# Keys made once and kept in device memory, instead of key-norm products and folded queries

## The reference, cut to what matters

```python
xn = layer_norm(x, g_norm)
q = xn @ Wq                                   # 128 -> 1024
k, v = jnp.split(ctx @ Wkv, 2, axis=-1)       # 128 -> 1024 each
q, k, v = map(split_heads, (q, k, v))         # 16 heads of 64
k = concat([null_key, k]); v = concat([null_value, v])
q = l2norm(q) * q_scale
k = l2norm(k) * k_scale
attn = softmax(einsum('bhid,bhjd->bhij', q, k) * 8.0)
out = einsum('bhij,bhjd->bhid', attn, v)
out = out.reshape(b, -1, 1024) @ Wout
return layer_norm(out, g_out)
```

## Time and profile before

| what | us |
|---|---|
| median of 3 runs | 1401.02 |
| profiled execution | 1405.52 |
| its span | 1403.7 |
| TensorE matmul busy | 1220.3 (87%) |
| DVE / ACT / POOL busy | 641.4 / 439.2 / 314.4 |
| mean granted TensorE clock | 0.892 of full |
| first to last key product, both cores | 50.5 to 524.2 |
| long block, first score product | at 803.3 |
| long block, end (copy of the last batch's output) | at 1321.2 |

### The profile page before, as it was taken

The page is one execution under the profiler, slowest core; times in us unless marked ns, Lnnn a source line. Parts: engine busy times, 40 slices in busy tenths (PEclk is TensorE's granted clock), DMA queues, the critical chain, the costliest instruction groups (busy, mean ns, idle before and its releaser), DMA issues.

```text
span 1403.7 us, 12934 instructions
## 1 busy us (share of the span) xinstructions
PE 1220.3 (87%) x4726; PEld 700.7 (50%) x4726; DVE 641.4 (46%) x1098; ACT 439.2 (31%) x550; POOL 314.4 (22%) x94
## 2 busy tenths in 40 slices
PE   7999578987779998776597899999999999999558
PEld 4666233744656662453486544454445444544534
DVE  2487573134459886222522343334334333433344
ACT  2466313331346552241110523322332232233011
POOL 0000000000000000000000066655663665566000
PEclk8999799985879998797588999999999999999569
DMA  8000000030000002005000000000000000000100
GB/s 349 42 1 1 0 0 0 1 120 0 1 0 1 0 1 90 0 1 224 1 1 0 1 15 19 19 16 16 19 19 12 19 19 16 15 19 7 64 3 7
DMA packets 21365, 40.02 MB, mean 29 GB/s; under 512 B 2496, under 2 KB 18880, under 8 KB 19648
## 3 DMA queue, kind: packets, MB, share of 16 engines
q1 hardware_dynamic: 21312, 39.30, 7.7%
HBM read 39.03 MB, written 0.26 MB: 28 GB/s over the span
## 4 chain that ended last, share of the span: by engine, by line
PE 80%; DVE 11%; ACT 6%; issue 2%; POOL 1%; DMA 0%; POOLq 0%; DVEq 0%; ACTq 0%
PE PSUM L1814 15%; PE PSUM L1818 15%; PE PSUM L1389 8%; PE PSUM L1460 3%; PE PSUM L1421 3%; PE PSUM L1398 2%; PE PSUM L1451 2%; PE PSUM L1549 2%; PE PSUM L1560 2%; PE PSUM L1415 2%; PE PSUM L1843 1%; PE PSUM L1849 1%; DVE ARENA L867 1%; PE PSUM L1924 1%; PE PSUM L1745 1%
## 5 line engine op out<-in xcount | busy, mean ns | idle before, releaser
L420 POOL TENSOR_TENSOR ARENA<-ARENA 128x2048 f32<-128x2048 f32 x64 | 288.7, 4512 | 196.2 <-ACT ARENA L654 196.2
L1230 DVE TENSOR_TENSOR ARENA<-PSUM,RK 128x512 f32<-128x512 f32 x256 | 175.7, 691 | 271.6 <-PE PSUM L1814 269.3
L1814 PE MATMUL PSUM<-ARENA,CK 128*128 128x512 f32 x512 | 257.3, 606 | 5.1 <-DVE ARENA L1230 4.3
L1818 PE MATMUL PSUM<-ARENA,CK 128*128 128x512 f32 x512 | 252.8, 597 | 5.8 <-ACT ARENA L676 3.7
L654 ACT ACTIVATE ARENA<-ARENA,CK 128x2048 f32<-128x2048 f32 x64 | 128.1, 2002 | 349.7 <-DVE ARENA L1230 349.7
L1818 PEld LDWEIGHTS PSUM<-ARENA,CK 128*128 128x128 f32 x512 | 97.6, 191 | 131.7 <-issue 113.2
L1814 PEld LDWEIGHTS PSUM<-ARENA,CK 128*128 128x128 f32 x512 | 97.6, 194 | 126.2 <-issue 97.7
L363 POOL TENSOR_TENSOR RSTD<-VE,MHALF 128x4 f32<-128x4 f32 x17 | 17.2, 1009 | 614.8 <-DVE VE L721 614.8
L1389 PE MATMUL PSUM<-WK,CT 128*128 128x512 f32 x256 | 122.9, 603 | 0.0
L450 ACT ACTIVATE SQ<-PSUM 128x512 f32<-128x512 f32 x128 | 76.3, 597 | 72.4 <-PE PSUM L1389 64.6
L743 DVE TENSOR_REDUCE RK<-SQ 128x8 f32<-128x512 f32 x128 | 84.1, 681 | 14.6 <-ACT SQ L450 12.5
(11 more groups left out here) (362 smaller groups left out, 1518.1 us busy)
## 6 DMA issues: line engine op xcount, KB each, us to landing
CT<-in_ctxT SPq DMA_DIRECT2D x4, 1024.0 KB, 10.4
CK<-in_l0f_experts SPq DMA_DIRECT2D x1, 4096.0 KB, 23.5
CK<-in_ctxk SPq DMA_DIRECT2D x1, 4096.0 KB, 12.5
ARENA<-in_l2f_experts SPq DMA_DIRECT2D x2, 2048.0 KB, 8.3
CK<-in_ctxT SPq DMA_DIRECT2D x64, 64.0 KB, 1.8
CK<-in_ctxr SPq DMA_DIRECT2D x64, 64.0 KB, 1.9
ARENA<-in_l2f_experts SPq DMA_DIRECT2D x1, 3072.0 KB, 14.3
WB<-in_wb SPq DMA_DIRECT2D x1, 2738.5 KB, 11.2
```

Source lines behind the costliest of these rows:

```text
L420: nc.gpsimd.tensor_tensor(LS[b % 2], LS[b % 2], PR[:, k % 2, :], ALU.add)\
L1230: ve.tensor_tensor(PR[:, k % 2, c * 512:(c + 1) * 512].rearrange("p (j n) -> p j n", j=4), PSUM[:, c % 2, :].rearrange("p (j n) -> p j n", ...
L1814: mm(bank(c % 2), CTT[:, k, :], qpb[:, b, c * 512:(c + 1) * 512], start=True, stop=True)\
L1818: return mm(bank(4 + c), CKT[:, k, :], PR[:, k % 2, c * 512:(c + 1) * 512], start=first, stop=final, skip_group_check=True)
```

## The change: what it does

The keys are now made, turned (feature on the partition, context row along the free axis), and kept.

- In the two cores, a key product is now weights by context (128 features of two heads x 512 rows). There are again 64 per core, but in the first 14 groups: five in each of the first eight, four in the next six (`key_plan`). The scalar engine copies each to one of four buffers, SP writes it to device memory (256 KB each, 32 MB in all), and GpSimd squares it. TensorE adds the squares over the partitions by products with a selection matrix: four products of 512 columns with 32 weight columns each, to four partition ranges of bank 0, for every four keys (`add_squares`), and turns the sums for every eight (`turn_norms`). The scalar engine copies them before and after. The vector engine has no part in it.
- In the long block, SP reads the keys back, 2 MB for every four tiles, into two buffers. A tile's scores are 16 products of 64 partitions and 128 columns, a pair of heads on partitions 0 to 63 and 64 to 127 writing to different banks. Value rows are made for each tile (two products of 128 x 512), copied half by the vector, half by the scalar engine. The values are summed by 16 products of 128 partitions and 128 columns with 64 weight columns, a pair of heads writing to partitions 0 to 63 and 64 to 127 of a bank. The exponential is done in two halves.
- The products with the folded key weights, the gather of raw rows, the value and turn steps at a batch's end and the raw tiles' DMAs are gone. A batch is closed by four products of 512 columns for the sums, two reciprocals of 512 and a multiplication of 1024 on the vector engine, and `Wout`. The null key is scored by 16 products of 512 columns ahead of the first tile, and its values open each batch's sum with four products of one partition.
- All loops are written out. The double norm becomes one statistic and two powers (`norm_twice_dve`). Some buffers move, and some signals share a name.

```diff
-    mm(bank(5 + 2 * c), CT[:, t * P:(t + 1) * P], WK[:, c * 512:(c + 1) * 512],
-        start=True, stop=True).then_inc(sem("key_rows"), PE.sends("key_rows"))
+def key_rows(units):
+    for n in units:
+        if n >= 2:
+            nc.tensor.wait_ge(sem("keys_kept"), n - 1)
+        mm(bank(5 + 2 * (n % 2)), WK[:, (n % 8) * P:(n % 8 + 1) * P], CT[:, (n // 8) * 512:(n // 8 + 1) * 512],
+           start=True, stop=True).then_inc(sem("key_rows"), PE.sends("key_rows"))
+def add_squares(halves):
+    for h in halves:
+        nc.tensor.wait_ge(sem("key_squares"), 4 * h + 4)
...
+        for j in range(4):
+            last = mm(PSUM[32 * j:32 * j + 32, 0, :], w("l3x_pick")[:, 32 * (h % 2):32 * (h % 2) + 32],
+                      KSQ[(4 * h + j) % 6], start=h % 2 == 0, stop=h % 2 == 1, skip_group_check=True)
...
+def key_squares(n0):                       # GpSimd
+    for n in range(n0, n0 + 64):
+        nc.gpsimd.wait_ge(sem("keys_kept"), n + 1)
+        if n >= 6:
+            nc.gpsimd.wait_ge(sem("key_squares_added"), (n - 6) // 4 + 1)
+        nc.gpsimd.tensor_tensor(KSQ[n % 6], KEEP_T[n % 4], KEEP_T[n % 4], ALU.mult)\
+            .then_inc(sem("key_squares"), PO.sends("key_squares"))
+def keep_keys(units):                      # scalar engine
+    for n in units:
+        nc.scalar.wait_ge(sem("key_rows"), n + 1)
+        if n >= 4:
+            nc.scalar.wait_ge(sem("key_squares"), n - 3)
+            nc.scalar.wait_ge(sem("dma_keys%d" % (n % 4)), 16 * (n // 4))
+        act(KEEP_T[n % 4], bank(5 + 2 * (n % 2)), ACT.Copy).then_inc(sem("keys_kept"), AC.sends("keys_kept"))
...
+def scores(t):                             # TensorE, long block
+    b, g = t // KEY_TILES, t // 4
+    if t % 4 == 0:
+        nc.tensor.wait_ge(sem("dma_keys_back%d" % (g % 2)), 16 * (g // 2 + 1))
+    for half in range(2):
+        if t:
+            nc.tensor.wait_ge(sem("l3x_scores_taken"), 4 * (t - 1) + 2 * half + 2)
+        for j in range(4):
+            c = 4 * half + j
+            for i in range(2):
+                last = mm(PSUM[:, 2 + 2 * half + i, j * P:(j + 1) * P],
+                          KG[DH * i:DH * (i + 1), g % 2, c, (t % 4) * P:(t % 4 + 1) * P],
+                          QSC[DH * i:DH * (i + 1), c, b * P:(b + 1) * P], start=True, stop=True)
+        last.then_inc(sem("l3x_scores"), PE.sends("l3x_scores"))
+def values(t):
+    nc.tensor.wait_ge(sem("l3x_probs"), 2 * t + 2)
...
+    for c in range(8):
+        for i in range(2):
+            at = ((c // 4) * 2 + i) * 512 + (c % 4) * P
+            last = mm(PSUM[DH * i:DH * (i + 1), 6 + c // 4, (c % 4) * P:(c % 4 + 1) * P],
+                      VT[:, t % 2, (2 * c + i) * DH:(2 * c + i + 1) * DH], PR[:, t % 2, at:at + P],
+                      start=False, stop=t % KEY_TILES == KEY_TILES - 1, skip_group_check=True)
+    last.then_inc(sem("l3x_values"), PE.sends("l3x_values"))
+scores(0)
+for t in range(TILES):
+    more = t + 1 < TILES
+    if more:
+        scores(t + 1)
+    if t > 1 and t % KEY_TILES == 1:
+        finish_out(t // KEY_TILES - 1)
+    if more:
+        value_rows(t + 1, 0)
+        value_rows(t + 1, 1)
+    if t and t % KEY_TILES == 0:
+        finish_sums(t // KEY_TILES - 1)
+    if t % KEY_TILES == 0:
+        null_values(t // KEY_TILES)
+    values(t)
...
+def finish_sums(b):                        # vector engine
+    nc.vector.wait_ge(sem("l3x_l"), b + 1)
+    ve.reciprocal(L9INV[:, 0:512], bank(0))
+    ve.reciprocal(L9INV[:, 512:1024], bank(1)).then_inc(sem("l3x_l_kept"), DV.sends("l3x_l_kept"))
+    nc.vector.wait_ge(sem("l3x_l_kept"), DV.sent("l3x_l_kept"))
+    nc.vector.wait_ge(sem("l3x_o_kept"), b + 1)
+    ve.tensor_tensor(OT8, OT8, L9INV, ALU.mult).then_inc(sem("l3x_o_ready"), DV.sends("l3x_o_ready"))
```

More of the change, by code:

```diff
@@ L305, in build, with key_plan, turn_of @@
         PICK2 = ARENA[0:16, 2048 + PAIRS * 3 * P:2048 + PAIRS * 3 * P + 16 * DH]
+        def key_plan(n0):
+            plan, n, added = [], n0, n0 // 4
+            for g in range(16):
+                first, second = (3, 2) if g < 8 else (2, 2) if g < 14 else (0, 0)
+                halves = list(range(added, n // 4))
+                halves = halves[:2 - added % 2]
+                turns = [h // 2 for h in (plan[-1][2] if plan else []) if h % 2]
+                plan.append((list(range(n, n + first)), list(range(n + first, n + first + second)), halves, turns))
+                added, n = added + len(halves), n + first + second
+            assert added == n // 4 and not plan[-1][2]
+            return plan
+        work_v, work_o = {}, {}
+        turns = [0]
+        def turn_of(table, at):
+            table[at] = turns[0] % 2
+            turns[0] += 1
+        turn_of(work_v, 0)
+        turn_of(work_v, 1)
+        for t in range(TILES):
+            if t > 1 and t % KEY_TILES == 1:
+                turn_of(work_o, t // KEY_TILES - 1)
+            if t + 1 < TILES:
+                turn_of(work_v, 2 * t + 2)
+                turn_of(work_v, 2 * t + 3)
+        turn_of(work_o, B - 1)
         block = ctx.enter_context(nc.Block())
@@ L453, in core_act @@
+            def core_act(groups, scale, plan=None):
                 for g in range(groups):
+                    first, second, halves, turned = plan[g] if plan else ([], [], [], [])
                     nc.scalar.wait_ge(sem("scores_shifted"), AC.due("scores_shifted"))
                     act(SX[:, g % 2, :], SX[:, g % 2, :], ACT.Exp, scale=scale).then_inc(sem("probs"), AC.sends("probs"))
[L456 to L457 removed]
+                    keep_norm_rows(turned)
+                    keep_keys(first)
@@ new lines, in _ @@
+            for t in range(TILES):
+                more = t + 1 < TILES
+                begins = more and (t + 1) % KEY_TILES == 0
+                ends = t and t % KEY_TILES == 0
+                if more:
+                    scale(t + 1, 0)
+                    scale(t + 1, 1)
+                if t and t % KEY_TILES == 1:
+                    finish_out(t // KEY_TILES - 1) if t > 1 else None
+                if more:
+                    value_rows(t + 1)
+                    scale(t + 1, 2)
+                    scale(t + 1, 3)
+                if begins:
+                    begin_sums((t + 1) // KEY_TILES)
+                if ends:
+                    finish_sums(t // KEY_TILES - 1)
@@ L1402, in core_pe @@
                 for g in range(groups):
+                    first, second, halves, turned = plan[g] if plan else ([], [], [], [])
                     if g + 1 < groups:
                         scores(g + 1)
-                    if norms_from is not None:
-                        key_norms_pe(norms_from + 4 * g, 2)
+                    turn_norms(turned)
+                    key_rows(first)
                     nc.tensor.wait_ge(sem("probs"), PE.due("probs"))
@@ new lines, in finish_sums @@
+            def finish_sums(b):
+                nc.tensor.wait_ge(sem("l3x_summed"), KEY_TILES * (b + 1))
+                take(0)
+                take(1)
+                for q in range(4):
+                    i = q % 2
+                    last = mm(PSUM[DH * i:DH * (i + 1), q // 2, :], w("ones")[:, 0:DH], LS[b % 2][:, q * 512:(q + 1) * 512],
+                              start=True, stop=True)
+                last.then_inc(sem("l3x_l"), PE.sends("l3x_l"))
+                freed[0] = freed[1] = ("l3x_l_kept", b + 1)
```

541 lines of the change are left out of this document (245 added, 296 removed).

## The result

The changed kernel takes 1354.95 us (median of 4 executions, 1347.57 to 1361.26) against 1401.03 for the kernel before (1400.99 to 1401.47). The ratio is 0.9668, with a 95% interval of 0.9618 to 0.9719. The profiled execution took 1356.67 us, its span 1354.6; the forecast for it was 1357, and 1353 for the median. Run again on another chip, the changed kernel took 1359.88 (1352.14 to 1362.19), the kernel before 1405.14 (1401.26 to 1409.51), ratio 0.9661 (0.9618 to 0.9705). So its spread of 10 us and more belongs to the kernel and not to one chip.

What follows compares the result with a forecast made beforehand. TensorE's stream was taken to bound the long block and both cores. The terms -65 - 22 - 9 - 4 - 3 + 29 + 26 = -48 gave 1357 us profiled, 1353 against the median of 1401.0; range 1308 to 1430.

Steps and rivals of the forecast that it cites:

- tile of the long block: Each long-block tile falls from 6.87 to 5.86 us, with short passes at 0.060 us each: -65 over 64.
- closing a batch: Long block, 3 times: sums and null values 3.8 us, TensorE waiting 5.2; together 9.0 against 16.2: -22.
- end: Long block, from the last addition to the end of the copy, 29.5 us before: -9.
- start: Long block's start: 15.6 us becomes 11.1, with null scores in pairs at 6.9: -4; unpaired +3.
- L0_xattn's core: Core's own work, keys, squares and turning 114.7 us, plus 5 of waits: 120 against 91, +29.
- L1_attn's core: This core, with changes between full and partial products, takes 121 us against 95: +26.
- The question on which all hung: Whether two TensorE products on different array halves run at once; overlap taken from a row showing only input-partition halves.
- Rival A: Products that differ only in their output partitions don't overlap: +141 us together, 1542; chance 0.15.
- Squares: In the cores, an addition takes 1.1 us and two changes between full and partial products, 1.3; 20.8 in all.
- Waits: In the cores, waits around GpSimd's squares and the scalar engine's copies: 0.3 us a group, 5 a core.
- C: Everything overlaps, but at 0.072 us a pass: long-block tile 6.62 us, kernel 1402; chance 0.15.
- D: In the cores, the ring of copy, square and addition binds: 20 us more in each, 1393; chance 0.06.

Runs made afterwards that it cites:

- the experiments on order: Changed kernel with only product order changed: scores half by half 1400.70 us, scores two by two 1366.11, value sums half by half 1439.62.
- the one on the squares' range: Changed kernel with the four products of each addition of squares all writing output partitions 0 to 31, not a range of 32 each: 1435.26 us.
- the fastest kernel: Changed kernel with closings spread over later tiles, last batch's end in halves with TensorE adding its probabilities, and a group's two additions of squares apart: 1329.82 us.
- the kernel with the additions apart alone: Changed kernel with a group's second addition of squares moved behind its value products, all squares on GpSimd: 1344.14 us.

## Why the prediction was right, point by point

| step | predicted | measured in the traces | |
|---|---|---|---|
| tile of the long block | 5.86 us, -65 | 5.80 us, -68 | short pairs ran at about 0.060 a pass |
| closing a batch | 9.0 us, -22 | 10.3, 8.6, 10.3 us, -19 | see below |
| end | 20.4 us, -9 | 18.6 us, -11 | see below |
| start | 11.1 us, -4 | 6.0 us, -10 | null scores 1.9 us and not 6.9 |
| double norms | -3 | -3.3 | |
| L0_xattn's core | +29 | +30.3 | |
| L1_attn's core | +26 | +31.4 | see below |
| sum | -48 | -50, and +1 in what is not named | the span fell by 49.1 |

The question on which all hung was answered as taken. Overlap across output partitions was chosen by the nearest row, though that row is of the other kind; the experiments on order and the one on the squares' range show that both kinds exist and what they are worth: 87 us for the values' half, 82 for the squares' quarters. Without either the kernel would have been slower than before. Rival A had been given 0.15, which was the risk of arguing from one kind to the other.

The answer was right for the two kinds of pair, but the total owes something to luck: single terms were off by up to 6 us, and they cancel.

*The closing.* Its 9.0 us left out the output products, 1.9 us at full clock, and took 5.2 us of waiting where 3.0 were measured (0.73 or 0.78, and 2.27); its own figures, 8 us less 2.4, give 5.5 or 5.6 rather than 5.2. Another 1.6 and 1.3 us are the half clock behind the wait, in two of the three.

*The end.* No run shows the 3.8 us at half clock that its 20.4 took for the sums: they took 1.94, at a granted clock of 1.00, which accounts for the 1.8 us between 20.4 and 18.6. The output products, behind a wait of 8.02 us, took 3.75 at 0.50.

*Squares.* 1.1 us and two mode changes, 1.3, was taken for an addition. It takes 1.0, and the change back shows in the two key products behind it, 1.91 us where two take 1.72 in the core's first group. So an addition costs 1.2 in all. By lines of the chain in L0_xattn's core, the additions have 16.2 us against the 20.8 forecast, the keys 58.0 against 55.0 (the changes back are in them), scores, transposes and values 37.8 against 35.5 (the first eight products of scores took 3.78 us in place of 2, at a granted clock of 0.50), the turning 3.6 against 3.4. The sum is 115.5 against 114.7, and it agrees in part because those 1.8 us at half clock made up for some of the squares.

*Waits.* 5 us a core were taken, 6.1 measured (122.61 - 116.48): 5.5 of them are the ring, as listed above, and 0.7 is a wait for a copy of the probabilities at the core's end. The place was foreseen (copy, square and addition in a circle), the event was not: it is the second of two additions, not a burst of keys.

*L1_attn's core* is the term that was most mis-sized: 121 us forecast, 126.7 measured. Of the 5.7 us, 2.6 are those of the first core too (122.6 against 120). The rest is that its groups are 0.28 us longer than the first core's, before and after (8.09 and 7.81 us). That makes 16 x 0.28 = 4.5 us; the prediction had it in the 95 us before and gave it 1 us after. The two stretches at half clock, some 2 us in the first core's start (0.50) and 1.6 behind a wait here (0.53), nearly balance.

*The range.* Its high end, 1430, doesn't follow from the words beside it: C and D together add 49 and 40 us, which is 1442. The measured time is far from both.

*The start* was mis-sized the other way. The null scores were counted in pairs. They differ in halves of the input and in quarters of the output at once:

```profile
849.23 1.99 PE L1891 MATMUL PSUM<-ARENA,WB 64*32 64x512 f32 x32
853.40 0.38 PE L1906 MATMUL PSUM<-ARENA 64*128 64x128 f32 x2 [2.19 <-ACT WB L698]
```

Thirty-two passes of 512 columns, 13.8 us in a row at 0.43, end in 1.99, some seven times as fast: eight passes start within 0.09 us, the next eight 0.45 later. There are eight pairs of a half and a quarter, and in the program two products of the same pair stand only two places apart. So by this reading (the records don't name the half here either) products started past others that had to wait, here past as many as six. The stage is 5 us shorter than forecast, which pays for L1_attn's core.

*What overlap and changes came to.* Two column ranges (the value sums) run 3.42 / 1.89 = 1.8 times as fast as passes in a row, with the change between full and partial products in it, and the four ranges of the squares 3.56 / 1.00 = 3.6 times. The score stream costs 1.98 - 16 x 0.107 = 0.27 over a perfect pair, all that a change and the pairing's loss together can be, and the key products behind an addition of squares take 1.91 - 1.72 = 0.19 longer. The 0.1 of the prediction was low for that change.

## What to carry to other kernels

Count TensorE's work in passes, and then ask of each product whether products close by in the queue use other partitions, of the input or of the output: that was worth a factor of 1.8 (value sums), 3.6 (squares) and seven (null scores) here, and in the scores and the values it hung on the order in which the loops issue them. A ring's wait has to be followed to the event that frees the slot before an engine is blamed for its pace: here a second engine for the squares gave 0.5 us a core, and moving one addition gave 3 to 4. When an execution varies by more than the effect, compare stages of the traces; a median 8 us lower was no evidence for an edit that had moved 1 us.

## What was not expected

- **Executions differ by up to 1% of the kernel's time, in stages that no edit touches.** On the first chip the kernel before varied by 0.5 us and the changed one by 14; on the second the kernel before went from 1401.3 to 1409.5 by itself, in the two later sets of runs from 1397.1 to 1409.7. The windows from the end of the first core to the start of the second, the same code in three executions (the kernel as changed, twice, and the one with the doubled writes):

```profile
168.76:456.45 287.69, 230.91 (x1026) 134.02 (x1027) 132.19 (x213) 94.75 (x134) 5.46 (x8) 0.82 0.04 15
```

```profile
169.78:460.41 290.63, 236.70 (x1026) 135.74 (x1027) 132.28 (x213) 95.19 (x134) 5.46 (x8) 0.80 0.04 15
```

```profile
171.75:452.21 280.46, 225.72 (x1026) 130.42 (x1027) 132.27 (x213) 94.76 (x134) 5.46 (x8) 0.84 0.04 16
```

  Granted clocks of 0.82, 0.80 and 0.84 and 287.7, 290.6 and 280.5 us. These stages are chains of short steps with waits between them: TensorE was busy for 230.9 of the 287.7 us, and the granted clock of the first of these executions was 0.62 from 168.76 to 200.00, 1.00 from 280 to 320 and 0.68 from 320 to 360. The tiles of the long block kept 5.80 us in all of them. What decides in which execution the clock falls was not found.
- **In the scores the overlap reached two products on, and needed no strict turn:** lower, lower, upper, upper costs 2.08 us a tile against 1.98, four and four 2.75.
- **Dense stretches lost clock too.** In the fastest kernel L1_attn's core had a granted clock of 0.96 and took 127.4 us, in the kernel with the additions apart alone 1.00 and 122.4, the same instructions; 5 us are left there. The first core of the changed kernel had 0.98 and 122.6 us in one execution, 0.96 and 125.3 in another.
